# A post-LN transformer block with gated FFN: the copies of the layer norm statistics on ScalarE, layer norm 2 issued at other places, the w_d load in two halves, a third PSUM bank

## The reference

```
h = layer_norm(x, ln1)                       # x: 4 x 4096 x 1024
q, k, v = h @ wq, h @ wk, h @ wv             # 4 heads of 256
q = softmax(q * s, over the head's features); k = softmax(k * s, over tokens)
context = k^T v;  attn = q context           # linear attention
a = x + attn @ wo + bo
h = layer_norm(a, ln2)
a = a + gelu(h @ w_ff1 + b_ff1) @ w_ff2 + b_ff2    # 1024 -> 4096 -> 1024
y = layernorm(x + a @ w_d + b_d)                   # "layer norm 3"
y = layernorm(y + (silu(y @ wg^T) * (y @ wu^T)) @ wd^T)   # hidden 3072, int weights / 127; "layer norm 4"
```

## Time and profile before

| | us |
|---|---|
| runs of the kernel before | 2050.20 and 2071.32, median 2060.76 |
| the profiled execution | 2052.28 |
| its span, slowest core (7) | 2050.1 |
| spans of the eight cores | 2037.5 to 2050.1 |
| mean granted TensorE clock, by core | 0.887 to 0.894 |

### The profile page before, as it was taken

The page is one execution under the profiler, slowest core; times in us unless marked ns, Lnnn a source line. Parts: engine busy times, 40 slices in busy tenths (PEclk is TensorE's granted clock), DMA queues, the critical chain, the costliest instruction groups (busy, mean ns, idle before and its releaser), DMA issues.

```text
span 2050.1 us, 20437 instructions; the slowest of 8 cores (2037.5 to 2050.1 us)
## 1 busy us (share of the span) xinstructions
PE 1608.5 (78%) x7096; PEld 678.7 (33%) x7096; DVE 637.6 (31%) x1004; ACT 475.8 (23%) x738; POOL 19.6 (1%) x26
## 2 busy tenths in 40 slices
PE   1488888996548366999999965556899999999562
PEld 0133333442213022444444421112344444444120
DVE  1633333202214532312122122444323223222445
ACT  1233333221211444031211302333210110011211
POOL 0000000000000000000000000000000000000000
PEclk9998998998789578999999986777899999999675
DMA  9321110020084300222222023102007006100112
GB/s 187 73 72 42 42 42 1 1 42 0 0 160 108 61 1 0 41 42 42 42 41 42 0 64 101 41 0 41 1 1 123 1 1 96 28 1 1 41 41 82
DMA packets 44067, 89.57 MB, mean 44 GB/s; under 512 B 832, under 2 KB 960, under 8 KB 43968
## 3 DMA queue, kind: packets, MB, share of 16 engines
q0 software_dynamic: 22880, 46.14, 14.1%
q1 hardware_dynamic: 21088, 42.13, 6.6%
HBM read 126.01 MB, written 8.39 MB: 66 GB/s over the span
## 4 chain that ended last, share of the span: by engine, by line
PE 52%; DVE 9%; ACT 4%; DMA 3%; issue 3%; DVEq 0%; ACTq 0%; SPq 0%; POOLq 0%
PE pb L816 11%; PE pb L790 11%; PE pb L981 8%; PE pb L1034 8%; PE pb L991 8%; PE pb L902 3%; DMA estR<-xkv 2%; PE pb L695 2%; ACT sbb L625 2%; PE pb L631 1%; DMA slotD<-wdd 1%; DVE R L865 1%; DVE R L945 1%; DVE xq L949 1%; DVE R L869 1%
## 5 line engine op out<-in xcount | busy, mean ns | idle before, releaser
L1034 PE MATMUL pb<-Dr,wslotE 128*128 128x512 bf16 x768 | 178.4, 396 | 28.2 <-DVE R L1041 28.2
L981 PE MATMUL pb<-h2x,W 128*128 128x512 bf16 x768 | 186.2, 386 | 4.8 <-ACT slbt L1000 4.8
L991 PE MATMUL pb<-h2x,W 128*128 128x512 bf16 x768 | 182.9, 381 | 0.0
L797 ACT ACTIVATE Gq<-pb,pv 128x512 bf16<-128x512 f32 x128 | 88.0, 687 | 301.8 <-PE pb L790 301.3
L1005 DVE SCALAR_TENSOR_TENSOR Dr<-slbt,pb 128x512 bf16<-128x512 bf16 x96 | 66.0, 688 | 270.9 <-PE pb L991 260.3
L831 DVE TENSOR_TENSOR R<-R,pb 128x512 f32<-128x512 f32 x96 | 66.0, 688 | 265.4 <-PE pb L816 265.4
L790 PE MATMUL pb<-h2x,W 128*128 128x512 bf16 x512 | 120.5, 399 | 31.3 <-ACT h2x L731 26.3
L1000 ACT ACTIVATE slbt<-pb 128x512 bf16<-128x512 f32 x96 | 57.3, 597 | 369.3 <-PE pb L981 366.0
L415 PE MATMUL pb<-W,h 128*128 128x512 bf16 x512 | 127.6, 394 | 0.4 <-ACT ebf L423 0.4
L431 PE MATMUL pb<-slotD,h 128*128 128x512 bf16 x512 | 121.7, 381 | 0.0
L1034 PEld LDWEIGHTS pb<-Dr,wslotE 128*128 128x128 bf16 x768 | 77.1, 101 | 127.7 <-issue 44.2
(11 more groups left out here) (93 smaller groups left out, 1425.0 us busy)
## 6 DMA issues: line engine op xcount, KB each, us to landing
xq<-xkv SPq DMA_DIRECT2D x8, 2048.0 KB, 11.2
estR<-xkv SPq DMA_DIRECT2D x8, 2048.0 KB, 17.6
W<-wff POOLq DMA_DIRECT2D x4, 2048.0 KB, 23.9
slotD<-wff POOLq DMA_DIRECT2D x4, 2048.0 KB, 17.6
y<-xq SPq DMA_DIRECT2D x4, 2048.0 KB, 6.9
W<-wgT POOLq DMA_DIRECT2D x3, 2048.0 KB, 16.9
W<-wuT POOLq DMA_DIRECT2D x3, 2048.0 KB, 28.6
wslotE<-wdT POOLq DMA_DIRECT2D x3, 2048.0 KB, 21.7
```

What stands on the lines that cost most here:

```text
L797: se = b.op("scalar", lambda e, jj=jj, t=t, qq=qq, bk=bk: e.activation(Gq[:, jj * NOWN + t * NT: jj * NOWN + (t + 1) * NT], bk["ap"][:, :] ...
L981: b.op("tensor", lambda e, hc=hc, kc=kc, t=t, bA=bA: e.matmul(bA["ap"][:, :], W0[:, kc * 1024 + hc * 128: kc * 1024 + (hc + 1) * 128], h2x ...
L991: b.op("tensor", lambda e, hc=hc, kc=kc, t=t, bB=bB: e.matmul(bB["ap"][:, :], W1[:, kc * 1024 + hc * 128: kc * 1024 + (hc + 1) * 128], h2x ...
L1034: b.op("tensor", lambda e, m=m, hc=hc, t=t, wds=wds, bk=bk: e.matmul(bk["ap"][:, :], wds[:, hc * 1024 + m * 128: hc * 1024 + (m + 1) * 128 ...
```

## The change

- In mk_ln's stats(), used by layer norms 2, 3 and 4, the bf16 copy is an activation (Identity) on ScalarE instead of a copy on VectorE. The square follows it on ScalarE, without a wait for VectorE.
- Layer norm 2 of tile 0: stats ahead of the attention output's tile 1, rows ahead of tile 2, bcs ahead of tile 3. Its l2_apply stays behind tile 3.
- Tile 1: stats and rows stay ahead of the FFN, bcs moves from there to t = 0, jj = 2 of its first quarter, l2_apply(1) from t = 0, jj = 4 to the start of t = 1.
- Tile 2: stats from t = 0, jj = 4 and rows from the start of t = 1, both to t = 1, jj = 2; bcs from t = 1, jj = 4 to jj = 6. Tile 3: stats and rows from t = 2, jj = 4 to jj = 2; bcs from the start of t = 3 to t = 2, jj = 6. l2_apply(2) and l2_apply(3) stay.
- w_d is loaded in two halves of its columns, gd1 and gd2, one after the other on POOL's queue; groups m = 0 to 3 wait for the first, 4 to 7 for the second. An element is 2 KB read and 1 KB written instead of 4 and 2.
- rot5 has three banks, 0 to 2, instead of two.

```diff
--- before.py
+++ after.py
@@ -620,14 +620,14 @@
                 xb = sbb[:, (c % 2) * 512:(c % 2) * 512 + 512]
                 xq_ = sbb[:, 1024 + (c % 2) * 512:1024 + (c % 2) * 512 + 512]
                 vw = list(extra_stat_waits) + [("te", ln_state[f"sbb_free{c % 2}"])]
-                ve1 = b.op("vector", lambda e, c=c, xb=xb: e.tensor_copy(
-                    xb, xsrc_c(c)), waits=vw, inc="ve")
+                ve1 = b.op("scalar", lambda e, c=c, xb=xb: e.activation(
+                    xb, xsrc_c(c), AF.Identity), waits=vw, inc="se")
                 ve2 = b.op("scalar", lambda e, xb=xb, xq_=xq_: e.activation(
-                    xq_, xb, AF.Square), waits=[("ve", ve1)], inc="se")
+                    xq_, xb, AF.Square), inc="se")
                 b.op("tensor", lambda e, xb=xb, c=c: e.matmul(
                     lnS["ap"][0:1, :], onescol, xb, start=(c == 0), stop=False,
                     skip_group_check=True),
-                    waits=[("ve", ve1)] + (Pool.w(lnS) if c == 0 else []))
+                    waits=[("se", ve1)] + (Pool.w(lnS) if c == 0 else []))
                 te = b.op("tensor", lambda e, xq_=xq_, c=c: e.matmul(
                     lnS["ap"][32:33, :], onescol, xq_, start=(c == 0), stop=False,
                     skip_group_check=True), waits=[("se", ve2)], inc="te")
@@ -684,10 +684,18 @@
     rot3 = mkpool([0, 1])
 
     x1_ve = [0] * 4
+    L2 = []
+    h2_ready = [0] * 4
     for t in range(4):
         slot = est.acquire()
         th, toff = slot["ap"]
         syv = load_x(th, toff, t * NT, waits=Pool.w(slot))
+        if t == 1:
+            L2[0]["stats"]()
+        elif t == 2:
+            L2[0]["rows"]()
+        elif t == 3:
+            L2[0]["bcs"]()
         for m in range(CH):
             bk = rot3.acquire()
             for kc in range(CH):
@@ -708,14 +716,10 @@
             Pool.rel(bk, "ve", ve)
         x1_ve[t] = b.cnt["ve"]
         Pool.rel(slot, "ve", x1_ve[t])
+        xsrc = lambda c, t=t: R1[:, c * NOWN + t * NT: c * NOWN + (t + 1) * NT]
+        L2.append(mk_ln(t, xsrc, "ln2", extra_stat_waits=[("ve", x1_ve[t])]))
     attn_all = b.cnt["te"]
     x0_read_ve = b.cnt["ve"]
-
-    h2_ready = [0] * 4
-    L2 = []
-    for t in range(4):
-        xsrc = lambda c, t=t: R1[:, c * NOWN + t * NT: c * NOWN + (t + 1) * NT]
-        L2.append(mk_ln(t, xsrc, "ln2", extra_stat_waits=[("ve", x1_ve[t])]))
 
     def l2_apply(t):
         ch = L2[t]
@@ -737,16 +741,12 @@
         Pool.rel(lnS, "ve", b.cnt["ve"])
         h2_ready[t] = b.cnt["se"]
 
-    L2[0]["stats"]()
-    L2[0]["rows"]()
-    L2[0]["bcs"]()
+
+    wslots = [W0, W1, slotD0, slotD1]
+    slot_free = [0, 0, 0, 0]
     l2_apply(0)
     L2[1]["stats"]()
     L2[1]["rows"]()
-    L2[1]["bcs"]()
-
-    wslots = [W0, W1, slotD0, slotD1]
-    slot_free = [0, 0, 0, 0]
     g_loads[1] = (load_w(wslots[2], wff1_d, FF, CH, col0=1024,
                          waits=[("te", attn_all)]),
                   load_w(wslots[3], wff2_d, D, CH, row0=1024,
@@ -766,22 +766,25 @@
         for t in range(4):
             if qq == 0:
                 if t == 1:
-                    L2[2]["rows"]()
+                    l2_apply(1)
                 elif t == 2:
                     l2_apply(2)
                 elif t == 3:
-                    L2[3]["bcs"]()
                     l2_apply(3)
             for jj in range(CH):
-                if qq == 0 and jj == 4:
-                    if t == 0:
-                        l2_apply(1)
+                if qq == 0:
+                    if t == 0 and jj == 2:
+                        L2[1]["bcs"]()
+                    elif t == 1 and jj == 2:
                         L2[2]["stats"]()
-                    elif t == 1:
+                        L2[2]["rows"]()
+                    elif t == 1 and jj == 6:
                         L2[2]["bcs"]()
-                    elif t == 2:
+                    elif t == 2 and jj == 2:
                         L2[3]["stats"]()
                         L2[3]["rows"]()
+                    elif t == 2 and jj == 6:
+                        L2[3]["bcs"]()
                 bk = rotA.acquire()
                 for kc in range(CH):
                     w = (Pool.w(bk) + [g1, ("te", g_read_te[t]),
@@ -849,12 +852,19 @@
             g_loads[nq] = (g1n, load_w(wslots[(2 * nq + 1) % 4], wff2_d, D, CH,
                                        row0=nq * 1024,
                                        waits=[("te", slot_free[(2 * nq + 1) % 4])]))
-    gd = load_w(slotD1, wdd_d, D, CH, waits=[("te", q3b_done[0])])
+    gd1 = gpQ.dma(lambda e: e.dma_start(
+        ap3(slotD1, 0, [[8192, 128], [1024, CH], [1, 512]]),
+        ap3(wdd_d, 0, [[D, 128], [128 * D, CH], [1, 512]])),
+        waits=[("te", q3b_done[0])])
+    gd2 = gpQ.dma(lambda e: e.dma_start(
+        ap3(slotD1, 512, [[8192, 128], [1024, CH], [1, 512]]),
+        ap3(wdd_d, 512, [[D, 128], [128 * D, CH], [1, 512]])),
+        waits=[("te", q3b_done[0])])
 
     est = Pool([(estR, 0), (estR, 4096)])
     est.items[0]["free"] = ("te", q3b_done[0])
     est.items[1]["free"] = ("te", q3b_done[0])
-    rot5 = mkpool([0, 1])
+    rot5 = mkpool([0, 1, 2])
     L3 = []
     x3s_ready = [0] * 4
     u_evac = [0] * 4
@@ -897,6 +907,7 @@
             L3[t - 1]["bcs"]()
         for m in range(CH):
             bk = rot5.acquire()
+            gd = gd1 if m < 4 else gd2
             for kc in range(CH):
                 w = (Pool.w(bk) + [gd, ("se", shv)]) if kc == 0 else []
                 b.op("tensor", lambda e, m=m, kc=kc, bk=bk, sh=sh: e.matmul(
```

## The result

| | before | changed |
|---|---|---|
| median of the executions timed together | 2069.82 us (of 39) | 2077.42 us (of 40) |
| lowest execution | 2050.04 | 2069.96 |
| profiled execution | 2052.28 | 2070.91 |
| spans of the eight cores in it | 2037.5 to 2050.1 | 2059.8 to 2069.1 |
| mean granted clock, by core | 0.887 to 0.894 | 0.875 to 0.879 |

The change makes the kernel slower by 0.6%: the ratio is 1.0059, with a 95% interval of 1.0039 to 1.0079. The two profiled executions stand 18.6 us apart and the two lowest ones 20 us, 0.9% to 1.0%. The ratio is smaller than that because it mixes two groups of executions. In the kernel before 23 of 39 lie at 2067 to 2073 us and 8 at 2050 to 2053.3; in the changed kernel 20 of 40 lie at 2070 to 2074.1 and 11 at 2080.7 to 2086.2.

The account below looks back on a forecast made before the run. It took TensorE, busy 78% of the span, as the bound, with its gaps to win or lose. Terms +13.1 +13.7 -6.5 -6.5 -0.7 gave +13.1 us on 2052.28, 2065.4, named 2066; forecast 2058 to 2074 (0.60), range 2054 to 2082.

Parts of the forecast that it names:

- The chances of leaving 2%: Whole kernel: outside 2011 to 2093 us, 0.05 for above and 0.01 for below.
- The copies, +13.1 in the tail and +13.7 in w_d: Layer norms 4 and 3: statistics passes, longer with copies on ScalarE, add 13.1 us in the tail and 13.7 in w_d.
- The model of the pass: Each statistics pass: ScalarE runs 16 instructions at 0.72 us in a row, 12.3 us instead of 8.9, 3.4 more.
- Rival 3: Statistics passes: each copy and square waits for its own matmul, 18.6 us per pass, 2134 us in all; chance 0.03.
- the relief of VectorE is worth nothing: All statistics passes: VectorE is waiting there, so 41 us less work on it gains nothing.
- the step that counts the same 3.4 us once for each tile: w_d stage: shad copies and rows stand behind the longer pass, so it counts three times; the fourth pass adds +3.4.
- The third bank, -6.5: w_d stage: one group instead of two left after layer norm's wait, -2.2 us for each of tiles 1 to 3.
- The halves, -6.5: w_d stage: first half lands after about 16 us, tile 0 ends near 1250 instead of 1256.8; taken as -6.5 us.
- Rival 2: w_d stage: both halves go ahead of the x loads, -18 us in place of -6.5, 2054 us in all; chance 0.13.
- equal bytes: w_d load beside x loads: its 27.49 us in the trace rather agrees with queues sharing by bytes than packet by packet.
- The head, -0.7: Attention output and layer norm 2: 6 us won at the FFN's start is given back, net -0.7, bounds -6 and +8.
- rival 1: Head: the new order takes tile 0's statistics, rows and broadcast off the path, -16.5 us, 2050 in all; chance 0.10.

Follow-up runs that it names:

- experiment 2: Kernel before with only the third bank (rot5) in the w_d stage: 2044.9 to 2048.0 us but for three longer executions, ratio 0.9969.
- experiment 1: Kernel before with only the statistics copies moved to ScalarE, at all three layer norms: 2087.25 to 2087.98 us, ratio 1.0142.
- Experiment 6: Changed kernel with the w_d stage's x load of tile 1 held until w_d's second half has landed: 2066.77 us, a single execution.
- experiment 4: Kernel before with only the new order of layer norm 2, copies left on VectorE: 2032.15 to 2033.3 us, ratio 0.9875.
- experiment 3: Kernel before with only w_d loaded in two halves: two levels, 2041.2 to 2045.8 and 2061.7 to 2066.3 us, ratio 0.9963.
- experiment 5: Changed kernel with the copies put back on VectorE: 2027.2 to 2028.3 us (one execution 2044.2), ratio to the kernel before 0.9887.
- experiment 9: Kernel before with the copies on ScalarE for layer norm 4 alone: 2060.5 to 2065.9 us and one execution 2082.5, ratio 1.0075.
- Experiment 8: Kernel before with the copies on ScalarE for layer norm 3 alone: 2060.5 to 2063.7 us, ratio 1.0055.
- experiment 12: Kernel of experiment 11 with layer norm 3's copies on ScalarE too: 1869.2 to 1871.9 us, ratio to the kernel before 0.9121.
- experiment 7: Kernel of experiment 5 with w_d loaded earlier, as one DMA into slotD0, and shad moved: 2010.4 to 2013.8 us, ratio to the kernel before 0.9791.
- experiment 10: Kernel of experiment 7 with layer norm work issued chunk by chunk between matmul groups, more banks, shad earlier: 1875.05 to 1877.1 us, ratio to the kernel before 0.9128.
- experiment 11: Kernel of experiment 10 with layer norm 4's copies on ScalarE: 1861.7 to 1863.7 us, ratio to the kernel before 0.9087.

## Why the prediction was right and wrong

**The time that I named.** The sum gave +13.1 us on the profiled 2052.28, and the profiled executions differ by 18.6, the stage means by 21.6: the sign was right, the size short by 30 to 40%. Term by term it was w_d +0.7 for a measured +4.2, head -0.7 for +2.5, gate 0 for +1.1 and tail +13.1 for +13.8. The named 2066 was wrong by 11 us against the median for a further reason. The step "this execution stands with the lower one; I name 2066" put the sum on the lower of two levels of the kernel before, 2050 and 2071, beside their middle, 2060.76, so that it reads as +5 us, a change too small to see. With 39 executions the median of before is 2069.82. The sum should have been told as a difference, +13 on whichever level: slower by 0.6%. That this is the ratio measured would have been luck: in the lower groups the kernels are 19 to 22 us apart (0.9% to 1.1%), and the ratio is smaller because it mixes the groups. The chances of leaving 2% (0.05 above, 0.01 below) were right in their letter and said nothing of the sign. Behind the size of the sum stand its terms. The one that was clearly mis-sized is the third bank, named as -6.5 and worth -3.5; the first half of w_d landed 5 us later than named, which cost 1 us of its term (-5.5 for -6.5); the head is told below.

**The copies, +13.1 in the tail and +13.7 in w_d.** Measured +13.4 to +14.2 and, with the gate, +14.2 to +14.6. The model of the pass held: 16 instructions at 0.72 us in a row. In the tail's first pass it is 12.6 us to the end of the last matmul for 12.3, and 3.7 more than before to the rows step for 3.4. Rival 3 would have shown 18.6 us. That the relief of VectorE is worth nothing held too, and so did the step that counts the same 3.4 us once for each tile because shad stands behind it on ScalarE.

**The third bank, -6.5.** Measured -3.5 from tile 1 to the gate (experiment 2), and -3.7 beside the longer passes (142.6 us in the changed kernel, 146.3 in experiment 1). The 2.2 us for the group that is no longer left over are in the chain, and tile 1 keeps them. The step that failed is that they pass to tiles 2 and 3 undiminished: their first four groups take 9.4 to 9.7 us where before they took 8.4 to 8.7 in tile 2 and, on five of the eight cores, some 8.5 in tile 3. Core 7, from which the prediction was read, had 9.95 there, so that on it the three tiles gave 1.8, 0.9 and 3.0.

**The halves, -6.5.** From the start of the wait to the last evacuation of tile 0: 1254.77 - 1215.54 = 39.2 us against 43.3 before, -4.1 core 5 against core 7. From the end of the FFN to the end of tile 0's matmuls the means over the eight cores are 38.3 and 43.7 us, -5.5, and -5.0 for the halves alone. I had the first half landing after 16 us; it came after 22.6 (20.2 to 22.6 on the eight cores). The step that failed counts it with the x load of tile 0 only. Experiment 6 shows the omitted term: the second x load shares the engines from the start, and without it the half lands after 13.6 to 18.1, mean 16.0: the term was right for one x load. I had the second one's 6.8 us in the total and left it out of the half. What kept the term near its size is that the bulk of the gain does not need 16 us: TensorE works through four groups while the second half comes in. Rival 2, the halves ahead of x, did not happen. Two readings of the prediction were wrong here. w_d did not come out last: on all eight cores x of tile 1 landed 1.2 to 2.3 us after it (1241.2 and 1243.3 on core 7). And the trace before does not rather agree with equal bytes: 513 packets of w_d passed beside 512 of x. That agrees with the rule of the Trainium skill that the prediction weighed (page "DMA: Bandwidth & Descriptors", section "Queues, rings and completion order"), that a DMA engine takes turns between the queues packet by packet.

**The head, -0.7.** The single times held best of all: 621.5 for 622.4, 692.9 for 692.9, 721.8 for 721.1, 767.1 for 765.5, 812.2 for 809.7, although on this core tile 0's last evacuation ended at 607.9 and not at 608.8. So did the reading that the gain at the start is given back because layer norm of the next tile now stands behind all eight gelus. What failed is the comparison: core 7 of before was one of the two at 252.9, where the mean is 249.9, so that the same times are a head of +2.5. Core for core (7 and 5) it is -0.1. And rival 1 was half true: the order alone takes 13.9 us off (experiment 4), close to its 16.5. I had judged the order only together with longer passes and so found nothing gained; the small sum hid a gain of 14 and a loss of 16.5.

**What the profile was to show.** ScalarE 60 us more busy: 61.0. TensorE's wait for w_d 16 us: 22.6, wrong. A second wait at m = 4: not on core 5, where the 64 matmuls of tile 0 run through in 16.19 us, but on core 0, whose chain of waits follows the second half:

```profile
1213.35 28.72 DMA slotD<-wdd
...
1242.20 7.08 PE pb L913 x32
```

One group instead of two: yes. The pass of 12.3 us: 12.6.

## What to carry to other kernels

Moving an instruction to an idler engine pays or costs by where it stands, not by busy shares: 32 copies cost 13 to 14 us where TensorE waited for the chain of copy and square, gained 12 us in a tail with the pass spread out and VectorE on the path, and cost 8 us in two stages where ScalarE had more to do and TensorE still waited for copy and square. Before such a move, cut the exposed pass itself: issuing it chunk by chunk between TensorE's groups, with the banks that this takes, gave 135 us, more than all other edits here together. And forecast a difference, not a level, and read each stage on all cores, for one core can stand 3.4 us from its neighbours in each.

## What the hardware showed that I had not expected

**A pair of cores at a clock of 0.81.** In the profiled executions of experiments 2, 3 and 5 two neighbouring cores run the first gated round at a granted clock of 0.81, neither of the two usual levels, for some 150 us, and the execution is 16 to 20 us longer. The longer executions of the kernel before (23 of the 39) and one of experiment 9 were not traced. Where such executions have spans by core, two neighbouring cores, in some two such pairs, end 16 us and more behind the others, at a mean clock of 0.874 to 0.882 where the others have 0.886 and more, as in the traced ones; I take them for the same. In the profiled execution of experiment 2 these were cores 0 and 1, with spans of 2064.4 and 2064.6 us against 2027.2 to 2042.7 of the others. Windows of core 0, in the stretch and behind it:

```profile
1470.00:1485.00 15.00, 15.00 (x59) 6.23 (x58) 2.75 (x4) 2.39 (x4) 0.00 (x0) 0.81 0.01 2
1590.00:1605.00 15.00, 15.00 (x71) 6.80 (x70) 5.89 (x9) 0.00 (x0) 0.00 (x0) 1.00 0.51 83
```

and of core 5 at the same time:

```profile
1470.00:1485.00 15.00, 15.00 (x72) 6.77 (x70) 3.28 (x5) 2.39 (x4) 0.00 (x0) 1.00 0.00 1
```

59 matmuls in 15 us, where the other core does 72: 0.82 of the rate. Core 0 needs 145.2 us for the first gate tiles, cores 2 to 7 126.4. The Trainium skill, page "TensorE: Matmul & The Clock Gate", section "Seeing it yourself", tells of a limiter that takes a whole die to 13/16 of the clock, 81.2%, once three of its cores run dense matmuls, and holds it while the load lasts. The level agrees with the 0.81 here. The rest does not: two cores showed it and their die's two others, as dense, stood at 1.00, and it went away under the same load. None of the traced executions with layer norm 3's copies on ScalarE has a pair at 0.81 (experiments 1, 6, 8, 12 and the changed kernel), but neither have those of the kernel before and of experiments 4, 7, 9, 10 and 11, and it is one execution of each. In the 11 executions of the changed kernel at 2080.7 to 2086.2 us one or two pairs were behind too, at a mean clock of 0.865 to 0.875; whether by the same stretch no trace shows. Experiment 8 was to ask whether the w_d stage decides it; its three short executions had no such pair, which is too few to say. What sets it off is open.

**Steps of 3.4 us between like cores.** The head took 246.1, 249.5 or 252.9 us on different cores of one execution, the w_d stage 199.6 or 203.0, in other kernels 192.5, 196.1 or 199.4 and 193.7, 197.2 or 200.5. One part of it can be seen in the clock. The first eight gate matmuls of the kernel before on core 6 (w_d stage 199.6) and on core 7 (203.0), chain of waits:

```profile
1408.88 1.83 PE pb L981 x8
```

```profile
1415.76 3.18 PE pb L981 x8
```

Core 6 enters the gate at the 2.4 GHz level, core 7 still at the lower one, and its first gate tiles take 127.7 us for 124.9. The tiles ahead differ too, 50.2, 47.7 and 37.6 us on core 6 for 48.8, 48.4 and 40.7. A saving of one or two microseconds can thus come out as nothing or as 3.4. What decides it for a core was not tried.

**A shorter burst, and not a slower pass, goes with a lower clock behind it.** In the changed kernel the four groups that open tiles 1 to 3 of the w_d stage take 9.5 to 9.9 us, where before tile 2's took 8.55. Two edits stand ahead of them, the longer passes and the third bank. Experiment 1 has the longer passes alone, and tiles 2 and 3 open as fast as before (core 7):

```profile
1344.56 8.53 PE pb L902 x32
...
1396.07 8.38 PE pb L902 x32
```

Experiment 2 has the third bank alone, with 9.38 and 9.52 us there, and 9.4 to 9.7 on the six cores whose matmul records are complete. So it goes with the bank, that is with a burst of 3.59 us instead of 5.5 to 6 ahead of the pass. In the kernel before tile 3 opened in 8.5 us on some cores and in 10.0 on others; what decides that was not tried.
